# Key tiles of 128 for 112 in a convolution and attention kernel, with one accumulator bank for each half of the queries and two banks for row maxima in place of three

## What is computed

```python
xs = (group_norm(xn) * gn_w + gn_b).reshape(B, 64, 784).transpose(0, 2, 1)
q, k, v = split((xs @ w_proj.T + b_proj).reshape(B, 784, 4, 48))   # 4 heads of 16
attn = softmax(einsum('bihk,bjhk->bijh', q, k) * 4, axis=2)        # over the 784 keys j
h = einsum('bjhk,bijh->bihk', v, attn).reshape(B, 784, 64) @ w_out.T + b_out
return x + h * sigmoid(h) + xs
```

## Time and profile before

| what | value |
|---|---|
| median of three runs | 1494.92 us |
| the profiled execution | 1497.84 us, its span 1496.0 us |
| granted TensorE clock, mean | 0.979 of full speed |
| matmuls (PE) busy | 1385.8 us, 93% |
| VectorE (DVE) busy | 1142.4 us, 76% |
| ScalarE (ACT) busy | 1053.1 us, 70% |
| GpSimd (POOL) busy | 408.9 us, 27% |
| chain of work that ended last, by engine | PE 40%, DVE 21%, issue 14%, DMA 12% |

### The profile page before, as it was taken

The page is one execution under the profiler, slowest core; times in us unless marked ns, Lnnn a source line. Parts: engine busy times, 40 slices in busy tenths (PEclk is TensorE's granted clock), DMA queues, the critical chain, the costliest instruction groups (busy, mean ns, idle before and its releaser), DMA issues.

```text
span 1496.0 us, 53539 instructions
## 1 busy us (share of the span) xinstructions
PE 1385.8 (93%) x23330; PEld 788.7 (53%) x23330; DVE 1142.4 (76%) x2461; ACT 1053.1 (70%) x1468; POOL 408.9 (27%) x300
## 2 busy tenths in 40 slices
PE   2999899999979999898999999999999999999996
PEld 1556466668853545454545455455554545545552
DVE  7778465556878888787879788888887888878863
ACT  3654477766632787777777777777777777877886
POOL 1410111101413215142251523505233151523110
PEclk9999999999987999999999999999999999999998
DMA  9000777750044173534637355372543636346322
GB/s 220 19 2 7 129 125 126 125 89 2 6 104 110 8 119 39 97 60 77 119 21 131 46 91 107 32 132 28 109 79 58 129 14 129 57 80 118 24 21 29
DMA packets 59266, 112.86 MB, mean 75 GB/s; under 512 B 20600, under 2 KB 45432, under 8 KB 58904
## 3 DMA queue, kind: packets, MB, share of 16 engines
q1 hardware_dynamic: 59032, 109.44, 44.3%
HBM read 54.23 MB, written 26.10 MB: 54 GB/s over the span
## 4 chain that ended last, share of the span: by engine, by line
PE 40%; DVE 21%; issue 14%; DMA 12%; SPq 7%; ACT 4%; POOL 2%; ACTq 0%; POOLq 0%; DVEq 0%
PE ps L1111 16%; DVE arena L1595 14%; DMA arena<-arena 7%; PE ps L1190 7%; PE ps L1016 6%; PE ps L989 4%; SPq L461 3%; ACT arena L904 2%; DMA k_dram<-arena 2%; PE ps L1034 2%; PE ps L1084 2%; PE ps L1170 2%; DVE bn L1310 1%; SPq L425 1%; POOL arena L652 1%
## 5 line engine op out<-in xcount | busy, mean ns | idle before, releaser
L1595 DVE TENSOR_REDUCE arena<-ps 128x1 f32<-128x392 f32 x1600 | 810.8, 559 | 156.8 <-PE ps L1111 156.4
L904 ACT ACTIVATE arena<-ps 112x784 f32<-112x784 f32 x896 | 698.2, 825 | 190.8 <-PE ps L1111 188.3
L1111 PE MATMUL ps<-arena 112*32 112x392 bf16 (+2 forms) x13312 | 696.2, 334 | 37.8 <-DVE arena L1595 17.9
L1111 PEld LDWEIGHTS ps<-arena 112*32 112x32 bf16 (+2 forms) x13312 | 358.0, 95 | 431.1 <-issue 117.9
L1190 PE MATMUL ps<-arena 112*32 112x392 f32 x3584 | 378.9, 493 | 0.3 <-ACT arena L904 0.3
L652 POOL TENSOR_TENSOR arena<-arena 128x784 f32<-128x784 f32 x31 | 57.9, 1869 | 561.5 <-DMA arena<-arena 561.5
L1016 PE MATMUL ps<-arena 96*64 96x392 f16 x1536 | 146.8, 334 | 8.8 <-ACT arena L783 8.4
L783 ACT ACTIVATE arena<-ps,arena 128x784 int16<-128x784 f32 x128 | 115.6, 912 | 48.9 <-PE ps L1016 46.3
L1190 PEld LDWEIGHTS ps<-arena 112*32 112x32 f32 x3584 | 114.6, 110 | 39.1 <-ACT arena L904 1.0
L1016 PEld LDWEIGHTS ps<-arena 96*64 96x64 f16 x1536 | 84.0, 110 | 60.6 <-ACT arena L783 21.5
L1517 DVE TENSOR_SCALAR arena<-arena 128x784 f16<-128x784 int16 x128 | 55.7, 435 | 78.2 <-ACT arena L783 76.6
(11 more groups left out here) (130 smaller groups left out, 951.7 us busy)
## 6 DMA issues: line engine op xcount, KB each, us to landing
arena<-arena SPq DMA_DIRECT2D x256, 84.2 KB, 2.8
arena<-q_dram SPq DMA_DIRECT2D x64, 294.0 KB, 4.8
arena<-k_dram SPq DMA_DIRECT2D x64, 294.0 KB, 4.6
q_dram<-arena SPq DMA_DIRECT2D x48, 196.0 KB, 6.7
k_dram<-arena SPq DMA_DIRECT2D x48, 196.0 KB, 4.1
x<-x_in SPq DMA_DIRECT2D x8, 784.0 KB, 21.0
out<-x SPq DMA_DIRECT2D x16, 392.0 KB, 5.2
arena<-arena SPq DMA_DIRECT2D x124, 49.0 KB, 6.0
```

What stands on the lines that cost most here:

```text
L904: nc.scalar.activation(probs[w % 2][:, 2 * pair:2 * pair + 2, :], two(2 * place, rows=slice(0, TT)), ACT.Exp).then_inc(s_taken, 1)
L1111: last = nc.tensor.matmul(to[at:end, :], stationary[:, at:end], moving, start=start, stop=stop, tile_position=(0, at))
L1595: v.tensor_reduce(mx[img % 2][:, c, unit:unit + 1], ps[:, max_bank(n), 0:CH], AX.X, ALU.max).then_inc(s_mf, 1)
```

## The change

- A key tile has 128 keys (`KT`) in place of 112. Six tiles cover keys 16 to 783; the first 16 keys of all four heads and both halves of the queries share one unit more, number 12 (`U_REST`). An image has 25 units in place of 28, and 50 groups of score matmuls in place of 56.
- There are still 14 weighs: twelve of the old kind and two of the rest, in units 14 and 15, where the four heads' strips of 32 rows lie on four row groups of the array (`tile_position=(32 * h, 32 * h)`). A table (`WEIGHED`) says which unit has which weigh.
- Each half of the queries has an accumulator bank of its own, 4 and 5; the row maxima keep banks 6 and 7 (`MAX_BANKS` 2). Every unit carries two chunks.
- `take_v` has eight copies in place of four, the last four of 16 partitions each.
- The statistics of pairs 13 to 15 move from layer 2's end into image 0 of attention (units 18, 20, 22); the later steps of attention's normalisation are spread over images 2, 3, 4, 5, 7 and 8 in place of 2, 4 and 6. One early piece of row maxima moves from step 17 to step 18.

```diff
-NU = NT * NH
-NW = NU // 2
+KT = 128
+NKT = T // KT
+KREST = T - NKT * KT
+NU = NKT * NH + 1
+U_REST = NU // 2
+NW = 2 * (NKT + 1)
...
-        NO_MAX = 0, 4, 22
...
-            return u not in NO_MAX and s + 1 + (nth_max(u) + AHEAD) // NM < B
+            return s + 1 + (u + AHEAD) // NM < B
...
-        BANK_ACC, BANK_MAX, MAX_BANKS = 4, 5, 3
-
-        def weighed(u):
-
-
-            return (u - 3) // 2 if u % 2 else None
-
-        U_ACC0 = 2 * (NT - 1) + 3
+        BANK_ACC, BANK_MAX, MAX_BANKS = 4, 6, 2
+
+        WEIGHED = {1: -1, 3: 0, 5: 1, 7: 2, 9: 3, 11: 4, 13: 5, 14: 6, 15: 7, 16: 8, 18: 9, 20: 10, 22: 11, 24: 12}
+        U_ACC0 = 14
...
-        EARLY_MAX = {16: (0,), 17: (1, 2), 18: (3,)}
+        EARLY_MAX = {16: (0,), 17: (1,), 18: (2, 3)}
...
+                for h in range(NH):
+                    rows = slice(32 * h, 32 * h + KREST)
+                    src = ps[rows, 2 * place + 1, 256:384].rearrange("p (i h d) -> p i h d", i=2, h=NH, d=DK)
+                    last = nc.scalar.activation(v_rest[rows, first:first + 2, 0:DK], src[:, :, h, :], ACT.Copy)
...
+                if u == U_REST:
+
+                    for c in range(2):
+                        for h in range(NH):
+                            last = nc.tensor.matmul(ps[32 * h:32 * (h + 1), 2 * place + c, 0:CH], k[0:ROWS_ALL, h, 0:32],
+                                                    q[0:ROWS_ALL, h, c * CH:(c + 1) * CH], start=True, stop=True,
+                                                    tile_position=(0, 32 * h))
...
-                jt = w % NT
+                c = int(w > NKT)
                 for h in range(NH):
-                    last = nc.tensor.matmul(ps[32 * h:32 * h + 32, BANK_ACC, 0:CH], vs[s % 4][:, jt, h, :],
-                                            probs[w % 2][:, h, :], start=(jt == 0), stop=(jt == NT - 1),
-                                            tile_position=(0, 32 * h))
+                    rows = slice(32 * h, 32 * (h + 1))
+                    if w in (NKT, NKT + 1):
+                        last = nc.tensor.matmul(ps[rows, BANK_ACC + c, 0:CH], v_rest[rows, s % 4, :],
+                                                probs_rest[rows, c, :], start=(c == 1), stop=(c == 0),
+                                                tile_position=(32 * h, 32 * h))
+                    else:
+                        jt = w - c * (NKT + 2)
+                        last = nc.tensor.matmul(ps[rows, BANK_ACC + c, 0:CH], vs[s % 4][:, jt, h, :],
+                                                probs[(c * NKT + jt) % 2][:, h, :], start=(w == 0), stop=(w == NW - 1),
+                                                tile_position=(0, 32 * h))
...
-                        if w == 0 and s >= 1 or w == NT:
-
-                            pe.wait_ge(s_acc, 2 * s + w // NT)
+                        if w in (0, NKT + 1) and s >= 1:
+
+                            pe.wait_ge(s_acc, 2 * s - 1 + w // (NKT + 1))
...
-                dve.wait_ge(s_v2, 2 * (q + 1))
-                stats(q)
...
+                if q < LATE_STATS:
+                    dve.wait_ge(s_v2, 2 * (q + 1))
+                    stats(q)
...
+                    if s == 0 and u in (18, 20, 22):
+                        p = LATE_STATS + (u - 18) // 2
+                        dve.wait_ge(s_v2, 2 * (p + 1))
+                        stats(p)
```

More of the change, by code:

```diff
@@ L268, in build @@
         AHEAD = 10
-        NO_MAX = 0, 4, 22
-        assert NU - len(NO_MAX) == NM
-        def nth_max(u):
-            return sum(k not in NO_MAX for k in range(u))
+        assert NU == NM
         def has_qk(s):
@@ L892, in l3 @@
                     elif what == "v":
-                        take_v(n, place, vs[(s + 2) % 4], vs[(s + 3) % 4])
+                        take_v(n, place, (s + 2) % 4)
                     elif what == "out":
@@ L1156, in v_product @@
             def v_product(place, halfway=lambda: None):
-                for t in range(NT):
-                    if t == NT // 2:
+                for t in range(NKT):
+                    if t == NKT // 2:
                         halfway()
-                    last = columns(ps[:, 2 * place + t // 4, (t % 4) * 128:(t % 4 + 1) * 128], TT,
-                                   xs[:, t * TT:(t + 1) * TT], P("wv"))
+                    at = KREST + t * KT
+                    columns(ps[:, 2 * place + t // 4, (t % 4) * 128:(t % 4 + 1) * 128], KT, xs[:, at:at + KT], P("wv"))
+                for h in range(NH):
+                    last = nc.tensor.matmul(ps[32 * h:32 * (h + 1), 2 * place + 1, 256:384], xs[:, 0:32], P("wv"),
+                                            start=True, stop=True, tile_position=(0, 32 * h))
                 last.then_inc(s_s, 1)
@@ L1176, in scores @@
             def scores(s, u, place):
[L1177 to L1182, removed]
+                q, k = qs[s % 4], ks[s % 4]
+                if u == U_REST:
+                    for c in range(2):
+                        for h in range(NH):
+                            last = nc.tensor.matmul(ps[32 * h:32 * (h + 1), 2 * place + c, 0:CH], k[0:ROWS_ALL, h, 0:32],
+                                                    q[0:ROWS_ALL, h, c * CH:(c + 1) * CH], start=True, stop=True,
+                                                    tile_position=(0, 32 * h))
+                else:
+                    c, jt, pair = tile_of(u)
+                    at = KREST + jt * KT
+                    for j in range(2):
+                        h = 2 * pair + j
+                        last = columns(ps[:, 2 * place + j, 0:CH], KT, k[0:ROWS_ALL, h, at:at + KT],
+                                       q[0:ROWS_ALL, h, c * CH:(c + 1) * CH])
```

84 lines of the change are left out of this document (53 added, 31 removed).

## The result

The changed kernel takes **1568.66 us** (median of 4 runs, 1567.38 to 1570.59) against 1494.50 for the kernel before: ratio 1.0482, 95% interval 1.0464 to 1.0501. The profiled execution took 1570.59 us with a span of 1568.8, so it is compared with the 1497.84 us (span 1496.0) of before: 72.8 us more, where the prediction's sum was 62. In the code after, the score and chunk matmuls are L1135, the weighs L1233, the rest's weighs L1228, the 25th row piece L1159, the exponentials L928, the reduces L1638, the statistics L1352.

A forecast was written before the change was run, and what follows sets the result against it. TensorE was taken to bound attention, VectorE 5% behind. Images 0 to 28 +52 us, last three +1, row-group shapes +7, before attention -1, image 0's statistics +3: 62 us on the profiled 1497.84, median 1557 us, range 1524 to 1590.

The forecast's parts named there:

- Two banks: Attention, second chunk of units without a weigh: 1.00 us loop makes TensorE stand 0.33 us, nine times, 3.0 us more per image.
- reciprocals' wait: VectorE's wait at the reciprocals in attention: taken as gone, 0.4 us less per image (0 to 0.43).
- Fewer groups: Attention on TensorE: 50 score groups per image in place of 56, 1.0 us less per image.
- The rest's weighs: Two weighs per image on four row groups: array shape changes cost 7 us in all, from nothing to 14.
- The sign named for this price: Shape changes in attention were to show as idle time before the two weighs of the rest, in their group.
- Second accumulator: Weighs in attention: no longer wait for ScalarE's copy, but no such wait stood there, so worth nothing.
- `take_v`: Four more small copies in every second image of attention: 0.5 us, 0.25 per image.
- End of layer 2: Three statistics and an aggregation leave the chain at layer 2's end: 4 to 5 us gained.
- Maxima ahead: 66 chunks ahead of attention on the two-bank loop: 6 us more, taken as 4 where products lie between.
- Statistics in image 0: Three statistics moved into attention's image 0, where VectorE's pause stops TensorE: 3 us more (0 to 4).
- The rivals: In attention: wait does not bite, 1468 us, chance 0.06; half the stand absorbed, 1510, 0.06; clock falls, 1630, 0.07.
- The check by columns: Attention: four times 392 columns at 2.4 GHz are 0.163 us, a weigh's eight 0.65, so TensorE streams almost without pause.

## Why the prediction was right, and where its sizes were off

The sum came out at 62 us for 72.8. By stretches of the two profiled executions, cut at first exponentials of images:

| stretch | forecast | measured |
|---|---|---|
| up to attention (475.00, now 481.61) | -1 | +6.6 |
| image 0 (30.26, now 36.79) | +5.0 | +6.5 |
| images 1 to 28 (898.2, now 954.0) | +56.6 | +55.8 |
| images 29 to 31 and the end (92.5, now 96.4) | +1.7 | +3.8 |

Each column is one execution. In five runs with the same order of work ahead of attention its first exponential comes at 476.3 to 481.6 us, and the change is the latest of them, so up to 5 of the 6.6 us in the first line can be a difference between executions.

- **Two banks.** Right in kind and size: loop 1.00 forecast, 1.01 to 1.02 measured; stand 0.33 and 0.34. Nine stands an image were counted, and the starts of an image of the shorter kind show nine. The third bank shortens such an image from 33.02 to 29.67 us, by 3.35. The longer kind falls from 34.62 to between 31.5 and 33.5 only, with the reciprocals' wait back. Over images 1 to 28 it is 2.86 an image, where the stands less that wait were put at 2.6.
- **Fewer groups.** No run has it alone, but the starts show it: in an image of the shorter kind the score groups fill 9.63 us before and 8.35 with three banks, 1.28 less for the 1.0 counted.
- **The rest's weighs.** The mis-sized term: 0.22 per image taken, bounds 0 to 0.44, measured 0.48. The nearest row, the transpose, priced a change at 0.11, and all four changes are paid at 0.12 each; taking half was without ground. The Trainium skill (TensorEngine Tiling (Array Packing), Tiling Modes, Key Properties) says that a change of the tiling mode drains TensorE. The trace agrees, with 0.10 us ahead of the weigh and 0.13 behind. That images 1 to 28 still came out at 55.8 us for 56.6 is luck in part: the weighs cost 0.26 more per image, and the fewer groups gave 0.28 more. The sign named for this price did not come: the group of these weighs has 0.0 us of idle time, and the price shows in the starts alone.
- **Second accumulator.** Nothing, as forecast.
- **The reciprocals' wait.** Forecast gone; in 640 to 1400 us no DMA wait of theirs is left, from 10.2 us.
- **`take_v`.** Four copies of 16 rows take 184 ns each, 0.74 us in two images, 0.37 per image at most for the 0.25 taken. Within the bounds; what of it lies on the path was not tried.
- **End of layer 2.** This term failed. I took 4 to 5 us gained; layer 2 takes 81.2 us for 82.7, and the statistics' removal is worth 1.5 at most. The chain of transform and addition over one pair of banks goes on at its own pace without them (the additions start 3.6 us apart in the rows of after, 430.55, 434.21 and 437.84, with VectorE idle for TensorE before each of the first two). A further 1.7 us lies ahead of layer 2's first addition, in code that did not change; that addition starts at 354.7 to 359.0 us in the runs of this document.
- **Maxima ahead.** From the end of the last addition to the first exponential 42.1 us for 35.7: +6.4 for +4. The sum of 6 ahead of its last step was right, in its prices and in its share of the low clock: two chunks take 1.02 at full clock (first two rows) and 1.20 at half (last two), and 44 of the 65 reduces there begin at half clock, the two thirds that were taken. What failed is the 2 us taken off for the products that lie between; no row stood for them.

```profile
453.57 0.82 PE L1135 MATMUL ps<-arena 112*32 112x392 bf16 x8 [0.34 <-DVE arena L1638]
454.59 0.82 PE L1135 MATMUL ps<-arena 112*32 112x392 bf16 x8 [0.20 <-DVE arena L1638]
...
460.16 1.03 PE L1135 MATMUL ps<-arena 112*32 112x392 bf16 x8 [0.15 <-DVE arena L1638]
461.36 1.03 PE L1135 MATMUL ps<-arena 112*32 112x392 bf16 x8 [0.16 <-DVE arena L1638]
```

- **Statistics in image 0.** 3 forecast, 3.7 measured.
- **The rivals.** The wait bites, and in the shorter images nothing absorbs it. The clock does not fall: TensorE stands 0.35 us in every 2.35, and the granted clock is 1.00 over 1075 us, from 484 us on; before, it fell to half at 621 us and again at 1127. The Trainium skill (TensorE: Matmul & The Clock Gate, A second HAM failure mode: psum-queue depth-cycling) would have the clock swing under such short, regular stands in a cycle over PSUM banks; this trace does not agree. In all traces of this document every fall in attention, but for those in a run's last 13 us, came with a single stand of TensorE, of 1.8 to 4.3 us.
- **The check by columns** does not come out as it is written: four times 392 columns at 2.4 GHz, one after another, are 0.65 us and not 0.163. The spacing of 0.167 means that the four strips run side by side; the eight matmuls of a weigh, in two rounds of strips, then fill 0.33 us a round. That the starts leave no pause holds by their spacing.
- Two small things stay open: 2 us of image 0 and the last images beyond the forecast were not traced to a cause.

## What to carry to other kernels

A buffer count between two engines is judged by a loop and a spacing: add up producer, consumer and both hand-overs, and compare with the time between the start of one piece and of the piece that reuses its buffer, at the place where the pieces stand closest, not on average. Where a buffer can't be had, spread the pieces evenly, and halve the work between them along the axis that the array runs through in time, not along strips that run side by side. When an engine gets faster, look for the step that it now reaches too early, and free what that step waits for before moving the step.

## What was not expected of the hardware

- Two column strips of fp32 weighs take as long as four, two passes 0.33 us apart, though their matmuls are half as many.
- 32 contraction rows cost as much as 128: the rest's weigh holds the array for 0.66 us on either, so the four row groups save no time and add the 0.23 us of the change.
- A 392 KB store issued 0.5 us ahead of a small DMA delays the engine that waits for the small one: moving the store halved that wait and made the program 0.7% faster.
- Nine regular stands of 0.34 us in an image left the clock at 1.00; four single stands of 1.9 to 2.7 us were each followed by 3.4 us at half clock.
